# Window attention plus expert block: probabilities transposed in 32x32 blocks by VectorE, moved by DMA, multiplied window by window

## The reference

```python
xn = layernorm(x)
# attention: windows of 64 rows, 16 heads of 32
qkv = xw @ qkv_w + qkv_b
attn = softmax(einsum('bnqhd,bnkhd->bnhqk', q, k) * scale + rel_pos_bias)
out = einsum('bnhqk,bnkhd->bnqhd', attn, v)
out = out.reshape(B, S, D) @ proj_w + proj_b
# experts: 8 of them, each takes its 1024 best rows by xn @ Wg.T
top_vals, token_idx = top_k(scores, 1024)
h = silu(xg @ W1[e].T) * (xg @ W3[e].T)
y = (h @ W2[e].T) * softmax(top_vals)
x = x + attention(xn) + scatter_add(y)
```

## Time and profile before

| | |
|---|---|
| median of three runs | 2057.91 us |
| profiled execution | 2061.68 us |
| span of its trace | 2059.9 us |
| TensorE busy | 1999.6 us, 97% |
| VectorE busy | 1157.6 us, 56% |
| ScalarE busy | 663.1 us, 32% |
| GpSimd busy | 597.2 us, 29% |
| mean granted TensorE clock | 0.991 |

### The profile page before, as it was taken

How to read it: one execution, slowest core, us unless ns; L and a number is a source line. 1 busy time by engine, 2 the same in 40 slices (tenths; PEclk the granted TensorE clock), 3 DMA queues, 4 the chain that set the end, 5 groups by cost and what they waited for, 6 DMA issues and landing times.

```text
span 2059.9 us, 36125 instructions
## 1 busy us (share of the span) xinstructions
PE 1999.6 (97%) x15051; PEld 1619.1 (79%) x15051; DVE 1157.6 (56%) x1748; ACT 663.1 (32%) x1015; POOL 597.2 (29%) x416
## 2 busy tenths in 40 slices
PE   6999999999999999998899999999999999999997
PEld 4777777787778788776788888888888888888886
DVE  5666677777768877676744544346344443444221
ACT  2333322323334443332433242232332333323221
POOL 1444444445444343353022021211212012111111
PEclk9999999999999999999999999999999999999999
DMA  7133334555432111212444253333532434325311
GB/s 209 68 106 100 105 109 122 146 164 167 141 91 63 55 30 42 63 63 87 159 104 111 72 134 91 65 105 87 131 79 62 124 81 107 92 66 143 62 21 21
DMA packets 152883, 198.17 MB, mean 96 GB/s; under 512 B 19376, under 2 KB 93488, under 8 KB 152752
## 3 DMA queue, kind: packets, MB, share of 16 engines
q1 hardware_dynamic: 138416, 162.77, 26.3%
q0 software_dynamic: 14336, 33.56, 9.1%
HBM read 128.13 MB, written 51.38 MB: 87 GB/s over the span
## 4 chain that ended last, share of the span: by engine, by line
PE 52%; DVE 0%; POOL 0%; ACT 0%; issue 0%; POOLq 0%
PE ps_e L59 17%; PE ps_e L61 17%; PE ps_e L60 17%; PE ps_e L157 1%; POOL out_rows L1649 0%; DVE xn L1802 0%; DVE xgt_lo L1807 0%; ACT x_res L1717 0%; DVE w_lo L1796 0%; DVE got L165 0%; POOLq L1648 0%
## 5 line engine op out<-in xcount | busy, mean ns | idle before, releaser
L59 PE MATMUL ps_e<-xgt_hi,w_hi 128*128 128x512 f32 x1024 | 404.4, 395 | 7.7 <-DVE xgt_lo L1807 7.7
L61 PE MATMUL ps_e<-xgt_hi,w_lo 128*128 128x512 f32 x1024 | 399.3, 390 | 0.0
L60 PE MATMUL ps_e<-xgt_lo,w_hi 128*128 128x512 f32 x1024 | 399.2, 390 | 0.0
L1828 DVE TENSOR_TENSOR hm<-ps_e,silu 128x512 f32<-128x512 f32 x128 | 88.4, 691 | 458.5 <-PE ps_e L61 457.7
L59 PEld LDWEIGHTS ps_e<-xgt_hi,w_hi 128*128 128x128 f32 x1024 | 192.7, 188 | 46.0 <-DVE xgt_lo L1807 8.2
L1649 POOL DMA_INDIRECT out_rows<-x_res,idx x64 | 100.6, 1572 | 432.6 <-ACT x_res L1717 418.2
L61 PEld LDWEIGHTS ps_e<-xgt_hi,w_lo 128*128 128x128 f32 x1024 | 192.8, 188 | 40.7
L505 POOL TENSOR_TENSOR pn_sb<-p_sb,s_rec 128x1024 f32<-128x1024 f32 x64 | 121.9, 1904 | 350.0 <-DVE s_rec L1186 281.5
L60 PEld LDWEIGHTS ps_e<-xgt_lo,w_hi 128*128 128x128 f32 x1024 | 192.9, 188 | 38.2
L59 PE MATMUL ps<-xt_hi,wqk_hi 128*128 128x512 f32 x512 | 215.2, 420 | 3.2 <-issue 2.3
L186 POOL DMA_INDIRECT x_in<-xn_rows,idx x64 | 74.4, 1162 | 486.8 <-DVE idx L178 308.8
(11 more groups left out here) (182 smaller groups left out, 3489.1 us busy)
## 6 DMA issues: line engine op xcount, KB each, us to landing
x_f<-in_w SPq DMA_DIRECT2D x48, 512.0 KB
raw<-in_w SPq DMA_DIRECT2D x48, 512.0 KB
x_res<-in_x SPq DMA_DIRECT2D x16, 1024.0 KB, 5.3
out_rows<-x_res SPq DMA_DIRECT2D x16, 1024.0 KB, 4.2
xn<-x_in SPq DMA_DIRECT2D x256, 64.0 KB, 2.0
xn_rows<-xt_plain SPq DMA_DIRECT2D x10, 1024.0 KB, 4.2
xn<-xn_rows SPq DMA_DIRECT2D x32, 256.0 KB, 5.3
x_in<-xn_rows SPq DMA_DIRECT2D x28, 256.0 KB, 4.6
```

The source lines that it names most:

```text
L59: nc.tensor.matmul(out, w_hi, x_hi, start=start, stop=False)
L60: nc.tensor.matmul(out, w_hi, x_lo, start=False, stop=False)
L61: return nc.tensor.matmul(out, w_lo, x_hi, start=False, stop=stop)
L1828: v.tensor_tensor(hm[:, m % 2, :], ps[:, 2 * (m % 2) + 1, :], silu[:, m % 2, :], ALU.mult).then_inc(hm_ready, 1)
```

## The change

Four things are changed together.

1. **Transposes.** For steps 0 to 61, `pn_sb` is written by GpSimd with the two 32-key halves apart (`halves_first`), VectorE transposes it in place in 32x32 blocks (`turn_probs`, one instruction of 128x1024), and SyncE carries the blocks to their partitions with eight DMAs of 32 partitions by 512 floats (`spread_probs`) into one of two buffers `pt`. The last two steps (62, 63) keep the transposes of TensorE and the copies.
2. **The product.** `pv` runs 32 matmuls over 64 keys and 64 query columns, one for each window and head; even and odd windows write different PSUM banks (`OT`, `OT2`).
3. **v** has two buffers.
4. **The pass.** PSUM banks are given out anew, and the chunk is written in four segments: (q, k, v0, v1, pv, scores), (q, k, v2, v3, pv, scores), (q, k, three output projections, gates, pv, scores), (one output projection, q, k, pv, scores). All engines' orders follow it. The start is written anew too: v weights are loaded before the later q and k weights, chunk 1's layernorm is transposed by TensorE as chunk 0's was (`first_xt(1)`), not by way of memory. In the last chunk the first expert's list is summed in two parts.

The diff, cut to the places that the prediction speaks of:

```diff
-        v_sb = sb("v_sb", [P, TT, C])
+        v_sb = [sb(f"v_sb_{i}", [P, TT, C]) for i in range(2)]
-        pn_sb = sb("pn_sb", [P, TT, 4, W])
-        pt_diag = sb("pt_diag", [P, TT, 4, P])
+        pn_sb = sb("pn_sb", [P, TT * 4 * W])
+        pt = [sb(f"pt_{i}", [P, 2, TT, 4, QD]) for i in range(2)]
...
-        SP, OT, QB, KB = 0, 4, 5, 6
+        SP, OT, OT2, QB, KB = 0, 4, 5, 6, 7
+        V_BANK, P_BANK, FINAL_BANK = (0, QB, 0, QB), (0, 1, QB, KB), (0, 1, 2, 3)
...
+            def spread_probs(s):
+
+                sp.wait_ge(pn_turned, s + 1)
+                if s >= 2:
+                    sp.wait_ge(o_mm, s - 1)
+                half = TT * 4 * QD
+                for w in range(2):
+                    for i in range(2):
+                        for j in range(2):
+                            src, dst = QD * (2 * w + i), QD * (2 * w + j)
+                            sp.dma_start(pt[s % 2][dst:dst + QD, i, :, :, :].rearrange("p t h q -> p (t h q)"),
+                                         pn_sb[src:src + QD, half * j:half * (j + 1)]).then_inc(pt_in, 16)
...
+            def normalise(s):
                 pool.wait_ge(rec_ready, s + 1)
...
+                    if s >= 1:
+                        pool.wait_ge(pt_in, PIECES * s)
+                    nc.gpsimd.tensor_tensor(halves_first(pn_sb[:, :]), p_sb[:, :, :, :].rearrange("p t h (j c) -> p (t h) j c", c=QD),
+                                            s_rec[:, :].unsqueeze(2).unsqueeze(3).to_broadcast([P, TT * 4, 2, QD]),
+                                            ALU.mult).then_inc(norm_ready, 1)
...
             def pv(s, m):
-                pe.wait_ge(pta_ready, s + 1)
-                pe.wait_ge(ptb_ready, s + 1)
...
+                    pe.wait_ge(pt_in, PIECES * (s + 1))
...
                 for t in range(TT):
-                    for h in range(4):
-                        col = HD * (4 * m + h)
-                        i = nc.tensor.matmul(ps[HD * h:HD * (h + 1), OT, P * t:P * (t + 1)],
-                                             v_sb[:, t, col:col + HD], pt_diag[:, t, h, :], start=True, stop=True)
+                    for w in range(2):
+                        keys = slice(W * w, W * (w + 1))
+                        for h in range(4):
+                            col = HD * (4 * m + h)
+                            i = nc.tensor.matmul(ps[HD * h:HD * (h + 1), (OT, OT2)[w], W * t:W * (t + 1)],
+                                                 v_rows[keys, t, col:col + HD], pt[s % 2][keys, :, t, h, :], start=True, stop=True)
...
+            def turn_probs(s):
+                dve.wait_ge(norm_ready, s + 1)
+                blocks = pn_sb[:, :].rearrange("p (b c) -> p b c", c=QD)
+                nc.vector.transpose(blocks, blocks).then_inc(pn_turned, 1)
```

TensorE's pass through one chunk as written now (`c` from 1 to 15; `lists_of` acts in chunk 15 alone, `hunt` in 10 to 14):

```diff
+                project_q(s, 0)
+                project_k(s, 0)
+                project_v(c, 0)
+                hunt(c, 1)
+                project_v(c, 1)
+                pv(s - 2, 2)
+                pe.wait_ge(v_ready, TT * c + 1)
+                slot_read(c, 1)
+                scores(s)
+
+                pe.wait_ge(v_ready, TT * c + 2)
+                project_q(s + 1, 1)
...
+                project_v(c, 3)
+                lists_of(2)
+                pv(s - 1, 3)
+                lists_of(3)
+                pe.wait_ge(v_ready, TT * c + 3)
...
+                scores(s + 1)
+
+                pe.wait_ge(v_ready, TT * c + 4)
+                project_q(s + 2, 2)
```

More of the change, by code:

```diff
@@ L556, in _ @@
             pool.wait_ge(const_in, 96)
[L557 to L558 removed]
             for c in range(1, NCH):
                 chunk(c)
[L561 removed]
+            subtract_max(G * NCH - 1)
+            residual(NCH - 1, (0, 1))
+            normalise(G * NCH - 1)
+            residual(NCH - 1, (2, 3))
         @block.scalar
@@ L734, in _ @@
             split_hi(0)
+            first_xt_hi(0)
             split_hi(1)
-            first_xt_hi()
-            for u in range(2, ALL_SPLIT):
-                split_hi(u)
+            split_hi(2)
             act.wait_ge(const_in, 96)
             nc.scalar.activation(q_bias[:, :], qk_bias[:, 0:G], ACT.Copy, scale=SCALE).then_inc(q_bias_ready, 1)
-            act.wait_ge(consts, 14)
             act.wait_ge(q_bias_ready, 1)
-            chunk(0, first=True)
+            q_part(0, 0)
+            split_hi(3)
@@ L1019, in chunk @@
-                if not first:
-                    pe.wait_ge(out_ready, TT * (c - 1) + 3)
-                hunt(c, 5)
-                if c + 1 < FAR:
-                    pe.wait_ge(gate_sb_ready, c + 2)
+                project_out(c - 1, 0)
+                if n < FAR:
+                    gate(n)
+                lists_of(4)
+                project_out(c - 1, 1)
+                if ahead:
+                    gate_ahead(j - 1)
+                hunt(c, 5)
+                lists_of(5)
+                project_out(c - 1, 2)
@@ L1100, in last_chunk @@
                     project_out_group(t, 3).then_inc(p_mm, 1)
-            pe.wait_ge(consts, 14)
-            first_xt()
-            chunk(0, first=True)
-            for c in range(1, NCH - 1):
+            pe.wait_ge(consts, 12)
+            first_xt(0)
+            first_chunk()
+            for c in range(1, NCH):
                 chunk(c)
-            last_chunk()
+            last_rows()
         @block.vector
@@ L1211, in layernorm_apply_ahead @@
                     dve.wait_ge(gatef_mm, j - FAR)
-                for t in range(TT):
+                for t in tiles:
                     nc.vector.tensor_scalar(by_quadrant(xt_f[:, t, :]), by_tile(x_f[:, t, :]), mv_f[:, t, 0:1], rstd_f[:, t:t + 1],
```

906 lines of the change are left out of this document (442 added, 464 removed).

## The result

| | before | after |
|---|---|---|
| median of 20 runs | 2058.7 us (2055.49 to 2061.96) | 2062.4 us (2058.0 to 2068.6) |
| ratio, 95% interval | | 1.002 (1.0012 to 1.0028) |
| profiled execution, its span | 2061.68, 2059.9 us | 2065.82, 2064.0 us |
| mean granted TensorE clock | 0.991 | 0.974 |

What follows compares the result with a forecast made beforehand. TensorE, busy 97% of the span, was taken as the bound. Its terms (−60 −10 −2 −12 +10 +5 +1 −4 = −72) took the profiled 2061.7 us to 1989.7, and the median, 3.8 lower, to 1986 us; range 1966 to 2030.

Steps and rivals of the forecast that it cites:

- Transposes, product, changeovers: On TensorE: transposes dropped in 62 steps −60 us, pv at 0.85 us −10, fewer changeovers between kinds of matmul −2.
- its own criterion (53.5): Chunks 1 to 3, where nothing is thin: the forecast is wrong if they are longer than 53.5 us.
- VectorE, cost 0: VectorE's transposes, 1.37 us a step, replace two copies of 0.69; cost 0, covered by its idle time.
- The start: Before step 3's scores: two waits go, 12 us, slower matmuls 3, TensorE's turning costs 3; −12, scores at about 64 us.
- (a): Chunks 5 to 9: first spread_probs queued on SyncE behind a 1 MB store and load; 2 us a chunk, +10.
- (b): Chunks 10 to 14: each take and prepare, 3.2 us a pair, stands before a v tile; net 1 us each, +5.
- The tail: Last scores to first expert matmul: step 62's transposes no longer stand behind six split products; −4 us (0 to −6).
- rival B: VectorE, GpSimd and transfers stay late: from chunk 4 on 3 to 4 us more a chunk, 2028 us; chance 0.20.
- A: Rival: the product does not get cheap, pv takes 1.6 to 2.0 us, total 2034 to 2061; chance 0.10.
- C: Rival: SyncE's issues become the bound; at 1.6 us each a chunk is 63 us, total about 2106; chance 0.05.
- D: Rival: pieces land in 3 us more often, waits at v's tiles vanish, start gains 18: 1970 us; chance 0.09.

Runs made afterwards that it cites:

- e8: The changed kernel without the carried pieces (pv reads a constant) and without the row maximum and its subtraction: 1996.1 us, 0.9698 of before.
- e5: The changed kernel without the row maximum and GpSimd's subtraction of it, pieces still carried: 2041.3 us, 0.9906 of before.
- e1: The changed kernel without its carrying transfers, pv reading a constant in pt: 2027.4 us, 0.984 of before.
- e6: The kernel before, without the row maximum and its subtraction: 2043.0 us, 0.9922 of before.
- e12: The changed kernel with two probability buffers, v's odd tiles in k's bank, later xt_lo, first pieces ahead of stores, and no row maximum: 2004.6 us.
- e9: The changed kernel with v's second and fourth tile made in k's PSUM bank instead of q's, from chunk 1 on: 2064.4 us, 1.0034 of before.
- e10: The changed kernel with GpSimd's xt_lo behind its subtraction of the maximum in chunks 10 to 14: 2060.6 us, 0.9999 of before.
- e17: The changed kernel without carrying, with v's odd tiles in k's bank and xt_lo later in chunks 10 to 14: 2022.2 us, 0.9812 of before.
- e16: The changed kernel with five mends, nothing left out, and x_res loaded through ScalarE's queue instead of SyncE's: 2069.5 us, 1.0054 of before.

## Why the prediction was wrong

- **Transposes, product, changeovers (−72): right.** e8 has chunks 1 to 4 at 52.3 us, the forecast's figure. As `pv` takes 0.79 us and not 0.85, 52.0 would have been due, so the agreement to the tenth is luck; to half a microsecond it is not. e5, which carries the pieces, has chunks 1 to 3 there too. With the carrying and the maximum in place chunks 1 to 3 take 53.6 to 53.9, already 1.4 us of new waits where the forecast saw nothing thin. By its own criterion (53.5) it was wrong here first.
- **VectorE, cost 0: wrong.** The transposes cost what was taken (1242 ns). But the cover, 11 to 13 us of idle time in a chunk, was counted as if it could be spent anywhere. VectorE runs in strict order and stands in a chain of four engines, and the shorter segments left that chain no reserve: leaving 3 us out of it gives 31 us back (e1 to e8, 2027 to 1996), and in the kernel before nothing in its steady chunks (e6). That edit also takes 4.9 us of VectorE's and 7.6 of GpSimd's work out of each chunk, so whether the length of the chain or the load on the two counts is not told apart. The forecast's proof that VectorE keeps in step was a chain of 9.2 us against segments of 10.0 and 12.8. (Its terms, 5.57, 1.5 and 1.9, add up to 9.0.) The chain takes 9.1 us only where nothing is late: the median is 10.5 in chunks 5 to 9 and 10.8 in chunks 10 to 13, above the last segment's 10.0. VectorE's instructions that wait beside GpSimd were not in the sum at all.
- **The start (−12): half right.** Step 3's scores run at 67.6 us, 9 earlier than before but not at 64. TensorE waits 7.3 us for the first pieces, which SyncE issues at 48.6, behind 16 small stores of chunk 1's rows (9.7 us). Step 0's pieces on SyncE's queue were never walked.
- **New waits, (a) +10: the mechanism right, the size wrong.** At 4.65 us less work a chunk, chunks 5 to 9 would be 268 us; they are 302, so +34. The carrying makes 24 of it (e1), not 10. The step took each landing 2.0 us after its issue, as for a piece alone. The median group of eight issues took 5.6 us, as forecast. But chunk 8's last piece landed 4.3 us after the last issue, behind a store and a load. The chunk began at 465.2, so the pieces were in 11.8 us later, where the forecast had 8 to 10; GpSimd had waited 6.6 us by then, not 2, and each such wait was handed on to GpSimd's only buffer, to VectorE and to TensorE, where the forecast added it once.
- **(b) +5: the step that failed most.** By the same reckoning chunks 10 to 13 would be 216 us; they are 255, so +39. One `take` and `prepare` was priced at 3.2 us. In chunk 10 the search's first preparation and three added terms put 6.6 us in front of a tile (600.10 to 606.74), where TensorE waited 8.8:

```profile
607.48 0.79 PE L59 MATMUL ps<-xt_hi,wqk_hi 128*128 128x512 f32 x1 [8.76 <-DVE v_sb L1249]
```

  Some 3.6 us of it are late pieces (without the carrying, in e1, the same wait is 5.2), and two of the three additions take 1.6 us instead of 0.7, beside GpSimd's additions to `x_res`. The fifth round came late through GpSimd.
- **The tail (−4): wrong.** From the last scores to the end it is 1.1 us longer. TensorE still waits 2.2 us for ScalarE's copy of the last step and 8.1 for the first expert's rows, where it was 7.7.
- **The clock.** The forecast named the loss of clock in rival B and priced it nowhere. TensorE's busy time in chunks 5 to 9 is 279 us against 5 x 53.55 in e8, some 11 us at a granted clock of 0.94 to 0.97; about as much in chunks 10 to 13 (224 against four of e12's 52.7 to 54.0).
- **The rivals.** A fell (0.79 us). B named the right mechanism, with 3.5 us a chunk too little: against the forecast's lengths chunks 5 to 9 are 5.4 us longer each and chunks 10 to 13 some 9. Of its two conditions, the slow multiplication did not come (1.9 us), the late landing did in part (2.3 us later, not 3). It should have had the larger chance, since the profile showed VectorE busy 46 of a planned 54 us in strict order. C fell: eight issues took 4.9 to 8.0 us, where C needed 11.6. D fell.

What stays open: how much of chunks 10 to 13 is the search's order and how much the shared port (e9 changes the first kind of place, e10 the second, e17 both, and the waits moved each time); how much of e1's 35 us are the transfers and how much `pv`'s freedom from the softmax, and why e16 was slower.

## What to carry to other kernels

- When work is taken off the bounding engine, walk the longest chain through the other engines at the new, shorter spacing, with buffers that are reused in place as part of it. Idle time on an engine that works in strict order is no cover for a wait that falls ahead of what the bounding engine wants next.
- If one mend after another shows nothing alone, the chain is late everywhere: measure first with its parts left out (e1, e8), to see what there is to win, and then mend several at once (e12 against e9 and e10).
- A transfer's price is its landing behind what its queue already holds, not that of one alone. A second queue alone did not help: in e16 the pieces landed later.
